# Last FFN, second pass: 16 instead of 14 pairs of units kept on chip, a quarter of the rounding and the bias moved to GpSimd, an eighth of the casts to ScalarE

## What is computed

```python
def _quant_per_tensor(x):
    scale = jnp.maximum(jnp.max(jnp.abs(x)), MIN_RANGE) / QP
    return (_ste_round(x / scale), scale)

def _qlinear(x2d, w, b):
    xq, sx = _quant_per_tensor(x2d)
    wq, sw = _quant_per_tensor(w)
    out = jnp.matmul(xq, wq.T) + b[None, :]
    return out * (sw * sx)
h = _qlinear(x.reshape(-1, D), w1, b1)
h = jax.nn.gelu(h, approximate=False)
o = _qlinear(h, w2, b2)
...
x = x + jnp.tanh(g_ffn[1]) * _L1_ffn_ref(_layernorm(x, axis=-1), ...)
```

## Time and profile before

| what | us |
|---|---|
| median of 3 runs | 1332.04 |
| lowest and highest of them | 1329.48, 1332.13 |
| the profiled execution | 1330.03 |
| its span, first to last instruction | 1327.9 |
| busy in the span: PE, DVE, ACT, POOL | 1200.3, 1121.6, 1014.3, 843.0 |

### The profile page before, as it was taken

The page is one execution under the profiler, slowest core; times in us unless marked ns, Lnnn a source line. Parts: engine busy times, 40 slices in busy tenths (PEclk is TensorE's granted clock), DMA queues, the critical chain, the costliest instruction groups (busy, mean ns, idle before and its releaser), DMA issues.

```text
span 1327.9 us, 30876 instructions
## 1 busy us (share of the span) xinstructions
PE 1200.3 (90%) x11618; PEld 854.3 (64%) x11672; DVE 1121.6 (84%) x1833; ACT 1014.3 (76%) x1732; POOL 843.0 (63%) x1313
## 2 busy tenths in 40 slices
PE   4699999999999999999967999998799888489898
PEld 3377777777777777777734666666667666244476
DVE  3488988998888889889877899988557999889898
ACT  2287887888888887888756999997455666699897
POOL 2147687877878687786773888776026686888000
PEclk9999999999999999999988999999999999699999
DMA  9577777767767776676310000001554453067199
GB/s 153 109 156 125 140 140 142 144 125 161 129 147 139 143 140 127 124 133 118 98 34 1 1 1 1 1 2 63 173 141 116 124 150 94 0 275 296 41 404 379
DMA packets 124963, 165.70 MB, mean 125 GB/s; under 512 B 47362, under 2 KB 78210, under 8 KB 120450
## 3 DMA queue, kind: packets, MB, share of 16 engines
q1 hardware_dynamic: 124048, 162.95, 51.4%
q10 hardware_dynamic: 768, 0.79, 0.5%
HBM read 76.07 MB, written 35.65 MB: 84 GB/s over the span
## 4 chain that ended last, share of the span: by engine, by line
PE 48%; DVE 15%; POOL 14%; ACT 12%; issue 6%; DMA 3%; SPq 2%; ACTq 0%; DVEq 0%; POOLq 0%
PE psum L591 8%; PE psum L606 7%; PE psum L578 4%; PE psum L566 4%; ACT f_gelu L2187 4%; PE psum L1049 3%; PE psum L636 3%; PE psum L618 3%; POOL rs L911 3%; ACT f_gelu L2179 3%; PE psum L1090 2%; PE psum L543 2%; POOL a_fac L1888 2%; PE psum L553 2%; DVE f_hid L1207 1%
## 5 line engine op out<-in xcount | busy, mean ns | idle before, releaser
L719 ACT ACTIVATE exp_t<-psum 128x512 f32<-128x512 f32 x512 | 278.6, 599 | 103.7 <-PE psum L591 103.7
L791 DVE TENSOR_REDUCE neg_max<-psum 128x8 f32<-128x1024 f32 x256 | 312.6, 1221 | 31.9 <-PE psum L578 24.0
L911 POOL TENSOR_TENSOR rs<-rs,minus_half 128x16 f32<-128x16 f32 x64 | 187.8, 2935 | 5.0
L591 PEld LDWEIGHTS psum<-q_stack,k_stack 50*128 50x128 f32 x2048 | 133.4, 186 | 75.8 <-ACT exp_t L719 41.6
L591 PE MATMUL psum<-q_stack,k_stack 50*128 50x128 f32 x2048 | 169.6, 285 | 1.4 <-ACT exp_t L719 1.4
L606 PE MATMUL psum<-exp_t,v_pad 128*32 128x256 f32 x2048 | 137.1, 385 | 0.7 <-ACT o_nt L729 0.4
L578 PE MATMUL psum<-k_stack,q_stack 48*128 48x256 f32 x1024 | 119.0, 310 | 18.5 <-DVE neg_max L791 15.3
L1049 PE MATMUL psum<-f_w,f_xqt 128*128 128x512 bf16 x482 | 118.4, 388 | 10.5 <-DVE f_hid L1207 3.4
L106 DVE BATCH_NORM_STATS2 norm_stats<-x_state 128x6 f32<-128x256 f32 x256 | 101.8, 411 | 11.5 <-DMA x_state<-in_x 11.5
L903 POOL TENSOR_TENSOR sq<-u 128x256 f32<-128x256 f32 x64 | 39.3, 614 | 108.9 <-DVE u L812 108.9
L1888 POOL TENSOR_TENSOR a_fac<-a_fac,a_expo 128x16 f32<-128x16 f32 x16 | 52.8, 3300 | 83.0 <-DVE a_fac L1794 82.6
(11 more groups left out here) (237 smaller groups left out, 3027.3 us busy)
## 6 DMA issues: line engine op xcount, KB each, us to landing
k_stack<-k_hi SPq DMA_DIRECT2D x252, 128.0 KB, 4.3
g_scratch<-f_gelu SPq DMA_DIRECT2D x18, 1024.0 KB, 5.1
k_stack<-k_lo SPq DMA_DIRECT2D x126, 128.0 KB, 4.6
f_gelu<-g_scratch SPq DMA_DIRECT2D x12, 1024.0 KB, 11.5
ctx_t<-in_ctx_t SPq DMA_DIRECT2D x32, 256.0 KB, 4.9
x_state<-in_x SPq DMA_DIRECT2D x16, 512.0 KB, 6.0
v_in<-in_ctx SPq DMA_DIRECT2D x32, 256.0 KB, 4.0
v_scratch<-v_in SPq DMA_DIRECT2D x32, 256.0 KB, 4.3
```

What stands on the lines that cost most here:

```text
L591: r = e.matmul(psum[:, 2 + j, o:o + P], self.k_st[rows, b // 2 % self.NK, pair // 2 % 2, pair % 2, i, pair // 4, b % 2, :], self.q_st[rows ...
L719: e.activation(self.prob[:, n % 3, j].rearrange("p n w t -> p (n w t)"), psum[:, 2 + j, :], ACT.Exp).then_inc(s["exp"], 1)
L791: e.tensor_reduce(self.negm[:, b % 2, :, :, 2 * u:2 * u + 2].rearrange("p j w n -> p j n w"), psum[:, 0:2, :].rearrange("p j (n w k) -> p ...
L911: e.tensor_tensor(self.rs[:, i], self.rs[:, i], self.expo[:, :], ALU.pow).then_inc(s["pool"], 1)
```

## The change

`RING` becomes 24 and `PLACED` 4, so 16 pairs (32 units) stay on chip and 16 are stored and loaded back (`NOUT` 18 to 16). The room comes from the bfloat16 tiles of b2, which go, from a smaller scratch for descriptors, and from places that are free late: the last pair has one unit in the weights' tile `f_w_up` and one in a piece of `f_xqt`. `ORDER` and the table `FREED` (in place of `BACK`) set which pair comes when and into whose slot it goes back.

In the second pass POOL rounds every unit with q % 4 == 1 (16 units) and ACT the other 48; ACT casts every unit with q % 8 == 5 (8 units) and DVE the other 56. The four bias matmuls per chunk go; POOL instead scales b2 once and adds it to x in 32 pieces of 128x512, ahead of DVE's `add`, which waits for it. POOL's `b2_parts` of the first pass goes.

```diff
-    H, NHT, CH, RING, EARLY = 1024, 8, 512, 22, 4
+    H, NHT, CH, RING, EARLY = 1024, 8, 512, 24, 4
-    PLACED = 3
+    PLACED = 4
...
+    ORDER = [4 * (7 - p) + i for p in range(4) for i in range(4)] + list(range(NOUT))
+    FREED = [r for r in range(NOUT + 1) if r != 3]
+    def rounded_by_pool(self, q):
+        return q % 4 == 1
+    def cast_by_act(self, q):
+        return q % 8 == 5
...
     def sp(self, w):
...
-                w.wait_ge(s["hq"], 2 * r + 2)
+                self.wait_cast(w, 2 * self.FREED[r])
+                self.wait_cast(w, 2 * self.FREED[r] + 1)
...
     def project(p):
-            for i in range(4):
-                e.matmul(psum[:, 4 * (p % 2) + i, :], self.ones16[0:65, :], self.b2_rows[0:65, :], start=True, stop=False)
...
     def act(self, w):
+        def round_off(q):
+            self.wait_rounded(w, q)
+            w.wait_ge(s["o_pe"], 11 * (q // 8 - 1) + self.COUNTED[q % 8])
+            g, shaped = self.unit(self.slot(q // 2), q % 2)
+            e.activation(shaped(self.hq[:, q % 8].rearrange("p j t -> p (j t)")), g, ACT.Copy, bias=-ROUND).then_inc(s["act_cast"], 1)
...
-        for q in range(self.NU):
-            rounded(q)
+        for q in range(self.NU + 1):
+            if q < self.NU and not self.rounded_by_pool(q):
+                rounded(q)
+            if q >= 1 and self.cast_by_act(q - 1):
+                round_off(q - 1)
...
     def dve(self, w):
         def add(p, i):
+            w.wait_ge(s["b2"], 4 * p + i + 2)
...
-            if q < self.NU:
+            if q < self.NU and not self.cast_by_act(q):
                 round_off(q)
...
     def pool(self, w):
+        def rounded(q):
+            self.wait_back(w, q)
+            g, _ = self.unit(self.slot(q // 2), q % 2)
+            e.tensor_scalar(g, g, self.m1[:, 5:6], ROUND, ALU.mult, ALU.add).then_inc(s["pool_rounded"], 1)
+        def add_b2(p, i):
+            b = 8 * self.chunk(p) + 2 * i
+            e.tensor_tensor(sh.x[:, b:b + 2, :], sh.x[:, b:b + 2, :], self.b2[:, :].unsqueeze(1).to_broadcast([P, 2, D]), ALU.add).then_inc(s["b2"], 1)
...
-            if j == 16:
-                b2_parts()
+        w.wait_ge(s["prep"], self.G_INV)
+        w.wait_ge(s["gmax"], self.NU)
+        rounded(1)
+        w.wait_ge(s["prep"], self.G_OUT)
+        w.wait_ge(self.fw.s["load"], self.fw.LOADED + 32)
+        e.tensor_scalar(self.b2[:, :], self.b2[:, :], self.m1[:, 6:7], 1.0, ALU.mult, ALU.mult).then_inc(s["b2"], 1)
+        w.wait_ge(s["b2"], 1)
+        for q in range(4, self.NU + 4):
+            if q < self.NU and self.rounded_by_pool(q):
+                rounded(q)
+            if q % 2 and (q - 5) // 2 < 4 * (self.NC // 2):
+                add_b2((q - 5) // 8, (q - 5) // 2 % 4)
```

More of the change, by code:

```diff
@@ L1987 @@
     X_MAX, X_ROW, X_SCALE, X_INV, M1, B1, G_MAX, G_ROW, G_SCALE, G_INV, G_OUT = 1, 2, 3, 4, 5, 6, 7, 8, 9, 10, 11
-    BEFORE_GATES = (143072 - 138048) // 4
-    ORDER = (list(range(NU // 2 - 4, NU // 2)) + list(range(NU // 2 - 8, NU // 2 - 4)) + list(range(NU // 2 - 12, NU // 2 - 8))
-             + [NOUT, NOUT + 1, NOUT - 2, NOUT - 1] + list(range(NOUT - 2)))
+    BEFORE_GATES = (143072 - 136256) // 4
+    ORDER = [4 * (7 - p) + i for p in range(4) for i in range(4)] + list(range(NOUT))
+    FREED = [r for r in range(NOUT + 1) if r != 3]
     COUNTED = [1, 2, 3, 4, 5, 6, 7, 11]
-    BACK = [NOUT - 2, NOUT - 1] + list(range(NOUT - 2))
+    def rounded_by_pool(self, q):
+        return q % 4 == 1
+    def cast_by_act(self, q):
+        return q % 8 == 5
     def __init__(self, sh, ctx, a1, fw):
@@ L2034, in slot @@
         v = self.ORDER[r]
-        return self.own_slot(v) if v >= self.NOUT else self.slot(self.BACK.index(v))
+        return self.own_slot(v) if v >= self.NOUT else self.slot(self.FREED[v])
     def own_slot(self, v):
@@ L2047, in pair, with unit, wait_rounded, wait_cast @@
         return halves[:, :, 2 * n:3 * n] if k == 2 else halves[:, k, 0:2 * n].rearrange("p (u t) -> p u t", u=2)
+    def unit(self, i, u):
+        if i < self.SLOTS + self.PLACED - 1:
+            return self.pair(i)[:, u], lambda z: z
+        if u:
+            return self.w16[0][:, :].bitcast(F32), lambda z: z
+        halves = self.xqt[:, :, :, :].rearrange("p h b t -> p h (b t)").bitcast(F32)
+        return halves[:, :, 6 * self.CH:7 * self.CH], lambda z: z.rearrange("p (h t) -> p h t", h=2)
+    def wait_rounded(self, w, q):
+        pool = sum(self.rounded_by_pool(i) for i in range(q + 1))
+        w.wait_ge(self.s["pool_rounded"], NSEQ // 2 - self.EARLY + pool)
+        w.wait_ge(self.s["hr_act"], q + 1 - pool)
+    def wait_cast(self, w, q):
+        act = sum(self.cast_by_act(i) for i in range(q + 1))
+        on_dve = sum(self.turned_on_dve(j) for j in range(NSEQ // 2))
+        w.wait_ge(self.s["act_cast"], NSEQ // 2 - on_dve + act)
+        w.wait_ge(self.s["hq_dve"], q + 1 - act)
     def moved(self, w, n):
         w.wait_ge(self.s_move[n % self.NSEM], 16 * (n // self.NSEM + 1))
+    def wait_back(self, w, q):
+        v = self.ORDER[q // 2]
+        if v < self.NOUT:
+            self.moved(w, self.NOUT + v)
     def turned_on_dve(self, j):
@@ L2079, in sp @@
                 n = self.NOUT + r
-                w.wait_ge(s["hq"], 2 * r + 2)
+                self.wait_cast(w, 2 * self.FREED[r])
+                self.wait_cast(w, 2 * self.FREED[r] + 1)
                 self.moved(w, n - self.NSEM)
-                e.dma_start(self.pair(self.slot(r)), t["g_scratch"][self.BACK[r]].rearrange("p (u t) -> p u t", u=2)).then_inc(self.s_move[n % self.NSEM], 16)
+                e.dma_start(self.pair(self.slot(self.FREED[r])), t["g_scratch"][r].rearrange("p (u t) -> p u t", u=2)).then_inc(self.s_move[n % self.NSEM], 16)
         for r in range(2 * self.NC - 8, 2 * self.NC):
@@ L2130, in project @@
                         r = e.matmul(psum[:, 4 * (p % 2) + i, b * D:(b + 1) * D], self.hq[:, q % 8, t // 4, t % 4 * P:(t % 4 + 1) * P], w2[:, n, :],
-                                     start=False, stop=u == 7 and b == 1)
+                                     start=u == 0 and b == 0, stop=u == 7 and b == 1)
                     if u == 7 or i == 3:
@@ L2178, in gelu @@
             made = psum[:, 2 * (u % 3):2 * (u % 3) + 2, :].rearrange("p j t -> p (j t)")
-            e.activation(self.pair(self.own_slot(u // 2))[:, u % 2], made, ACT.Gelu, scale=self.m1[:, 3:4],
+            into, shaped = self.unit(self.own_slot(u // 2), u % 2)
+            e.activation(into, shaped(made), ACT.Gelu, scale=self.m1[:, 3:4],
                          bias=self.b1[:, u % 8:u % 8 + 1]).then_inc(s["gelu"], 1)
         def rounded(q):
[L2183 to L2187, removed]
+            self.wait_back(w, q)
+            g, _ = self.unit(self.slot(q // 2), q % 2)
+            e.activation(g, g, ACT.Copy, scale=self.m1[:, 5:6], bias=ROUND).then_inc(s["hr_act"], 1)
+        def round_off(q):
[3 more added lines that the diff above has]
+            e.activation(shaped(self.hq[:, q % 8].rearrange("p j t -> p (j t)")), g, ACT.Copy, bias=-ROUND).then_inc(s["act_cast"], 1)
         for u in range(-8, self.NU):
             if u % 2 == 0 and 0 <= u + 8 < self.NU and not self.turned_on_dve((u + 8) // 2):
-                e.activation(*self.turned(w, (u + 8) // 2), ACT.Copy, bias=-ROUND).then_inc(s["xt_act"], 1)
+                e.activation(*self.turned(w, (u + 8) // 2), ACT.Copy, bias=-ROUND).then_inc(s["act_cast"], 1)
             if u >= 0:
@@ L2213, in find_max @@
             w.wait_ge(s["gelu"], u + 1)
-            e.tensor_reduce(self.gmax[:, u:u + 1], self.pair(self.own_slot(u // 2))[:, u % 2], AX.X, ALU.max,
-                            apply_absolute_value=True).then_inc(s["gmax"], 1)
+            g, _ = self.unit(self.own_slot(u // 2), u % 2)
+            e.tensor_reduce(self.gmax[:, u:u + 1], g, AX.XY if len(g.shape) == 3 else AX.X, ALU.max, apply_absolute_value=True).then_inc(s["gmax"], 1)
         def round_off(q):
-            w.wait_ge(s["hr"], q + 1)
+            self.wait_rounded(w, q)
             if q >= 8:
                 w.wait_ge(s["o_pe"], 11 * (q // 8 - 1) + self.COUNTED[q % 8])
-            e.tensor_scalar(self.hq[:, q % 8].rearrange("p j t -> p (j t)"),
-                            self.pair(self.slot(q // 2))[:, q % 2], ROUND, None, ALU.subtract).then_inc(s["hq"], 1)
+            g, shaped = self.unit(self.slot(q // 2), q % 2)
+            e.tensor_scalar(shaped(self.hq[:, q % 8].rearrange("p j t -> p (j t)")), g, ROUND, None, ALU.subtract).then_inc(s["hq_dve"], 1)
         def add(p, i):
@@ L2278, in quantise @@
             w.wait_ge(s["prep"], self.X_INV)
[L2279 to L2295, removed]
+            e.tensor_scalar(self.xn[:, i:i + 2], self.xn[:, i:i + 2], self.m1[:, 2:3], ROUND, ALU.mult, ALU.add).then_inc(s["pool_rounded"], 1)
+        def rounded(q):
+            self.wait_back(w, q)
+            g, _ = self.unit(self.slot(q // 2), q % 2)
```

(4 more changed lines are left out.)

14 lines of the change are left out of this document (5 added, 9 removed).

## The result

| | before | after |
|---|---|---|
| median of 4 runs, us | 1331.89 | 1345.51 |
| lowest and highest | 1329.48, 1332.13 | 1342.52, 1347.02 |
| the profiled execution | 1330.03 | 1342.52 |
| its span | 1327.9 | 1340.7 |
| "pass": from the scale's reciprocal on DVE to the end of the last add | 71.2 | 86.3 |

The ratio after to before is 1.0104, with a 95% interval of 1.0091 to 1.0118: the change makes the kernel 13.6 us slower. The forecast was 1349, in a range of 1337 to 1359.

A forecast was written before the change was run, and what follows sets the result against it. ACT's pace bounded the second pass, DMA and PE close behind. POOL and DVE in turns end POOL at 78.2 us, DVE at about 90 against 71.15: 1330.0 + 19 = 1349 us, range 1337 to 1359.

The forecast's parts named there:

- ACT, PE, DMA, residency: Second pass: ACT falls to 58.2 us, PE to 58.9, DMA to 61.7; loads have cover enough.
- some 0.8: Sign in the second pass: the DMA share falls from 1.02 to some 0.8.
- The turns: Second pass: DVE casts and POOL instructions exclude each other; 1.53 us per rounding turn, 1.68 per add turn, 76.8 together.
- 15 x 1.53: Second pass: 15 POOL roundings, each in turn with one DVE cast (0.98 + 0.55 us), 23.0 us.
- 1358: Upper neighbouring value in us: no gain at the hand-over, turns of whole durations sum to 85.6 instead of 76.8.
- 9 casts and 8 adds: End of second pass: DVE work left after POOL, 10.7 us, plus 1.0 waiting for PE.
- near 1.5: Sign in the second pass: POOL's roundings have a mean near 1.5 us in place of 1.12.
- 1.6 apart: Sign in the second pass: starts of DVE's casts lie about 1.6 us apart.
- 1, side by side: Second pass: DVE and POOL run at the same time, so the kernel gets faster, 1324 us; chance 0.07.
- 2, only the roundings exclude: Second pass: POOL's b2 adds pass beside casts, only roundings exclude them; no change, 1331 us; chance 0.03.
- 3, PE loses its clock: Second pass: PE falls to 1.2 GHz, a unit takes 1.79 us, 1373 us in all; chance 0.04.
- 4, casts first: Second pass: casts always get the ports first, POOL's lead is lost; within the forecast's range, no separate chance.

The follow-up runs named there:

- e3: The changed kernel with ACT rounding and DVE casting all 64 units, POOL only scaling b2 and the bias left out; 1329.81 us, ratio 0.9985.
- e1: The changed kernel without POOL's 32 adds of b2, its 16 roundings kept and the bias left out of the result; 1328.37 us, ratio 0.9953.
- e2: The changed kernel with DVE's casts from unit 8 on cut to 8 of 1024 columns, all else kept; 1328.6 us, ratio 0.9979.
- e5: The changed kernel with POOL doing only its b2 adds, ACT rounding and DVE casting all 64 units; 1347.82 us, ratio 1.0137.
- e4: The changed kernel with the bias matmuls back on PE, so that POOL only rounds; 1328.59 us, ratio 0.9984.

## Why the prediction was right, and where it was off

**ACT, PE, DMA, residency.** As forecast none of them holds the end. A cast on ACT was put at the pace of a rounding, 1.04; the instruction behind it starts 0.96 us after it (it takes 1.06, a rounding 1.13), and ACT stands for POOL's roundings. The DMA share over the whole pass falls from 0.95 to 0.78. The forecast set its "some 0.8" against the 1.02 of the middle, and there it only fell to 0.98. e3 shows the residency worth nothing by itself.

**The turns.** The deciding term came from one pair of rows and held: a POOL add in its turn was put at 1.68, its starts lie 1.69 apart. The Trainium skill, "SBUF — State Buffer", section "SBUF: two separate sides", calls the port pair an exclusive lock for whole instructions. The trace agrees on the exclusion, with 1.20 for a cast of 0.68; on the length the measurement decides: whole durations in turn, 1.87 for an add and a cast in the sum behind 1358, are longer than the 1.69 that was measured, and the hand-over of the rows, 1.68, fits it.

**Roundings, the term that was too small.** "15 x 1.53" took one cast per rounding. That holds for seven of the 15: they take 1.56, and the next instruction starts 1.53 after them. The other eight let two casts pass and take about 2.07; the mean of all 15 is 1.83, by the starts some 4 us more in all. POOL ended 82.6 us after the release, 4.4 behind the 78.2 forecast.

**The end, off the other way.** The forecast left 9 casts and 8 adds for DVE after POOL, 11.7 us. But 47 turns and eight second casts make 55 of the 56 casts, and only the last cast and the last four adds were left: DVE ends 3.8 us after POOL, 8 us less. The two misses have one cause, the second casts, and together (+4.4 and -8) they are the 3.7 us between the 90 forecast for the pass and the 86.3 measured; another 2.2 us by which the profiled execution lies under the forecast come from the start-up. That the one miss made up for half of the other was not foreseen: it is luck that the number lies so near.

**The signs.** Means of 1.71 (adds) and 1.21 (all casts, "over 1.2") and DVE's gapless row came as told; roundings "near 1.5" did for every second one only; starts of casts "1.6 apart" did not, 7 casts go in 10.3 us, 1.47 each. POOL's last instruction ends at 1334.0, 2 us later than told, and DVE's last add at 1337.8, 6 us earlier than told.

**The rivals.** 1, side by side: out by e1 and e2. 2, only the roundings exclude: out by e5. 3, PE loses its clock: the granted clock is 0.99 over the pass. 4, casts first: half true, for roundings (e4), not for adds (e5).

## What to carry to other kernels

Before work goes to POOL, look in the trace for one of its instructions beside the DVE form that it would meet, and compare both durations with what they take alone; what is added to busy shares is the turn, not the instruction. Here 59 us of POOL work and 54.7 us of DVE work fit on paper and made 86.3, while DVE's add with an input from PSUM paid nothing. Count the price per moved instruction on the engine that was near its limit: one POOL add cost DVE's path 0.44 to 0.8 us, and all that it saved was a matmul of 0.26 (8.2 / 32).

## What the runs showed of the hardware that was not expected

- A POOL rounding (tensor_scalar, float32) does not get its turn after one cast each time: in the change two casts passed it in eight cases of 15, always where the next cast stood right behind the running one; in e4 once four casts (3.33 us). It is no rule that it waits for a run of casts to end: at the head of e4's pass roundings were let in after two, with a third behind. POOL's add (tensor_tensor) never lost a second turn: of 32 in e5 the longest took 1.73. Why the two differ stays open; no run changed only the kind of instruction at the same place.
- A cast of 8 columns still waits its turn: in e2 the 42 on `f_gelu` have a mean of 0.60 us, the shortest 0.156.
- Two executions of programs that are the same up to the first L719 reached it 1.9 us apart. A span is worth less than a stretch between two events of one profile.
